# Layer 0 attention scores in 32-row tiles of TensorE, with queries and keys laid out per head through DRAM

## The reference, cut to what matters

```
xn = layernorm(x)
q = xn @ Wq.T ; k = xn @ Wk.T ; v = xn @ Wv.T        # q: 256 wide, k and v: 64 wide
qh = q.reshape(b, s, 4, 8, 8)                        # 4 queries per kv head, 8 heads, head width 8
kh = k.reshape(b, s, 8, 8)
scores = einsum('bsqhd,bthd->bqhst', qh, kh) * 8**-0.5
a_dot = einsum('bqhst,bthd->bsqhd', softmax(scores), vh)
sigma_q = elu(q) ; a_mem = sigma_q @ memory / (sigma_q @ memory_norm)
x = x + a_dot * (1 - w) + a_mem * w + ffn(xn)        # ffn: 256 -> 2048 -> 256, 4-bit weights
```

## Time and profile before

| | |
|---|---|
| median of the timed runs | 842.98 us |
| the profiled execution, its own time | 845.34 us |
| its span, first to last instruction | 843.4 us |
| PE busy | 741.0 us (88%), 5602 matmuls |
| PEld busy | 637.2 us (76%) |
| DVE busy | 632.9 us (75%) |
| ACT busy | 468.3 us (56%) |
| POOL busy | 424.2 us (50%) |
| mean granted TensorE clock | 0.953 of 2.4 GHz |

### The profile page before, as it was taken

The page is one execution under the profiler, slowest core; times in us unless marked ns, Lnnn a source line. Parts: engine busy times, 40 slices in busy tenths (PEclk is TensorE's granted clock), DMA queues, the critical chain, the costliest instruction groups (busy, mean ns, idle before and its releaser), DMA issues. The chain is left out here.

```text
span 843.4 us, 15160 instructions
## 1 busy us (share of the span) xinstructions
PE 741.0 (88%) x5602; PEld 637.2 (76%) x5602; DVE 632.9 (75%) x1099; ACT 468.3 (56%) x746; POOL 424.2 (50%) x369
## 2 busy tenths in 40 slices
PE   3368799999999999999999999999788898889773
PEld 2256678888888887888888888888666687777562
DVE  6989877787777676677768768665264898989865
ACT  4246645655655665564665565657675555565411
POOL 2344354354356566657535434436546373764821
PEclk9579999999999999999999999999979999999985
DMA  5111121111011010110100000021100000000000
GB/s 157 28 39 39 39 77 47 35 50 46 3 33 38 23 40 24 49 40 26 27 10 14 22 2 21 21 78 39 40 14 0 1 1 26 1 26 1 1 26 25
DMA packets 22108, 25.89 MB, mean 31 GB/s; under 512 B 4498, under 2 KB 17170, under 8 KB 22036
## 3 DMA queue, kind: packets, MB, share of 16 engines
q1 hardware_dynamic: 22036, 24.93, 10.4%
HBM read 14.83 MB, written 3.28 MB: 21 GB/s over the span
## 5 line engine op out<-in xcount | busy, mean ns | idle before, releaser
L652 DVE TENSOR_REDUCE neg_max<-s_pair 128x4 f32<-128x1024 f32 x127 | 154.9, 1220 | 75.5 <-PE s_pair L866 75.3
L474 ACT ACTIVATE probs<-t_pair 128x1024 f32<-128x1024 f32 x128 | 131.3, 1025 | 136.4 <-PE t_pair L891 136.2
L371 POOL TENSOR_TENSOR hid<-g,hid 128x512 f32<-128x512 f32 x64 | 82.1, 1283 | 177.8 <-DVE g L763 144.7
L365 POOL TENSOR_TENSOR hid_lo<-hid,hid_hi 128x512 fp32r<-128x512 f32 x64 | 85.5, 1336 | 82.8 <-ACT hid_hi L497 82.7
L866 PE MATMUL s_pair<-K,Q 96*128 96x256 f32 x508 | 85.0, 291 | 15.6 <-DVE neg_max L652 9.3
L866 PEld LDWEIGHTS s_pair<-K,Q 96*128 96x128 f32 x508 | 75.8, 195 | 24.2 <-issue 8.1
L891 PE MATMUL t_pair<-Q,K 104*128 104x512 f32 x256 | 86.2, 418 | 0.3 <-DMA Q<-max_parts 0.3
L933 PE MATMUL down<-hi,hid_hi 128*128 128x256 f32 x256 | 83.9, 328 | 0.8 <-POOL hid_lo L365 0.8
L906 PE MATMUL misc<-probs,V 128*32 128x256 f32 x1024 | 69.4, 389 | 3.3 <-DVE kc L608 2.6
L933 PE MATMUL down<-lo,hid_hi 128*128 128x256 f32 x256 | 71.5, 279 | 0.0
L933 PE MATMUL down<-hi,hid_lo 128*128 128x256 f32 x256 | 71.3, 278 | 0.0
(11 more groups left out here) (258 smaller groups left out, 1964.8 us busy)
## 6 DMA issues: line engine op xcount, KB each, us to landing
stage<-in_ternary SPq DMA_DIRECT2D x18, 256.0 KB, 2.8
Q<-q_hi SPq DMA_DIRECT2D x64, 64.0 KB, 2.0
stage<-in_scales SPq DMA_DIRECT2D x8, 384.0 KB, 3.4
X<-in_x SPq DMA_DIRECT2D x8, 256.0 KB, 4.2
Q<-q_lo SPq DMA_DIRECT2D x32, 64.0 KB, 2.0
Q<-max_parts SPq DMA_DIRECT2D x128, 4.0 KB
out<-X SPq DMA_DIRECT2D x8, 256.0 KB, 2.2
signs<-w_stage SPq DMA_DIRECT2D x9, 128.0 KB, 1.8
```

Source lines behind the costliest of these rows:

```text
L365: pool.tensor_tensor(hid_lo[:, m % 2, :, :].rearrange("p a n -> p (a n)"), hid[:, m % 2, :], hid_hi[:, m % 2, :, :].rearrange("p a n -> p ...
L371: pool.tensor_tensor(hid[:, m % 2, :], g[:, m % 2, :], hid[:, m % 2, :], ALU.mult).then_inc(S["hid_done"], 1)
L474: act.activation(probs[:, u % 2, th, :], t_pair[:], ACT.Exp, scale=SCALE).then_inc(S["probs_done"], 1)
L652: dve.tensor_reduce(neg_max[:, u % 2, 4 * jp:4 * jp + 4], score_banks(u, jp)[:].rearrange("p (s n) -> p s n", n=SEQ), AX_X, ALU.max, negat ...
```

## The change

Queries and keys are laid out per head. `Q[:, head, :]` and `K[:, head, :]` hold, for query r of the head, 24 rows from partition 32 r on, and two more rows for the maxima. A matmul reads only the 24 (or 26) rows of one block, a 32-row tile of the array, and `scores` and `scores_turned` issue their four matmuls so that two tiles alternate, each writing to a PSUM bank of its own. No rows of other heads take part, so the masks on POOL, `hq_mask` and `max_rows` go. `scores_turned` now covers two queries for all 256 keys with four matmuls of 256 columns, where it covered four queries for 128 keys with two of 512.

SBUF-to-SBUF copies cannot make that layout in few DMAs, so the parts of queries and keys are first stored to DRAM (`store_queries`, six DMAs, `store_keys`, one) and then loaded (`place_heads`, eight DMAs per quad, four for Q and four for K). The maxima of a unit are placed by four DMAs where there were two. The weights' columns are reordered on the host (`by_dim`).

```diff
-    for kind in ("stats", "norm", "turn", "q", "qlow", "kv", "qload0", "mask0", "qload1", "mask1"):
+    for kind in ("stats", "norm", "turn", "q", "qlow", "kv", "qstore", "kstore", "load0", "load1"):
...
-        for n, kind in (..., (4 + late, "qlow"), (4 + late, "qload0"), (4 + late, "kv"),
-                        (5, "mask0"), (5, "recip0"), (6, "recip1"), (8, "qload1"), (8, "mask1")):
+        for n, kind in (..., (4 + late, "qlow"), (4 + late, "qstore"), (4 + late, "kv"), (4 + late, "kstore"),
+                        (5 + late, "load0"), (5, "recip0"), (6, "recip1"), (8, "load1")):
...
-        Q = sb("Q", [P, 2, QPK, SEQ], F32R)
-        K = sb("K", [P, 2, QUAD, SEQ], F32R)
+        Q = sb("Q", [P, HEADS, SEQ], F32R)
+        K = sb("K", [P, HEADS, SEQ], F32R)
...
+            def store_queries(b):
+                sp.wait_ge(S["q_parts"], 3 * b + 1)
...
+                for part, x in ((0, q_hi), (2, q_hi), (1, q_lo)):
+                    if part == 1:
+                        sp.wait_ge(S["q_lo_done"], b + 1)
+                    for jj in range(2):
+                        dst = dram["q_parts"][b % 2, jj::2, DKV * part:DKV * part + DKV, :].rearrange("c e n -> e c n")
+                        sp.dma_start(dst.bitcast(F32), x[DKV * jj:DKV * jj + DKV, :, :].bitcast(F32)).then_inc(S["q_stored"], 16)
+            def store_keys(b):
+                sp.wait_ge(S["kc_lo_done"], b + 1)
...
+                sp.dma_start(dram["k_parts"][b % 2].bitcast(F32), kc[0:KROWS, :, :].bitcast(F32)).then_inc(S["k_stored"], 16)
+            def place_heads(b, quad):
                 if b > 0:
                     sp.wait_ge(S["st_done"], 2 * (HEADS * (b - 1) + QUAD * quad + QUAD))
+                heads = slice(QUAD * quad, QUAD * quad + QUAD)
+                sp.wait_ge(S["q_stored"], 96 * (b + 1))
+                for r in range(QPK):
+                    src = dram["q_parts"][b % 2, r].rearrange("(e h) n -> e h n", h=HEADS)[:, heads, :]
+                    sp.dma_start(Q[32 * r:32 * r + HROWS, heads, :].bitcast(F32), src.bitcast(F32)).then_inc(qk_placed[quad], 16)
...
+                sp.wait_ge(S["k_stored"], 16 * (b + 1))
+                for r in range(QPK):
+                    src = dram["k_parts"][b % 2].rearrange("(e h) q n -> e q h n", h=QUAD)[:, quad]
+                    sp.dma_start(K[32 * r:32 * r + HROWS, heads, :].bitcast(F32), src.bitcast(F32)).then_inc(qk_placed[quad], 16)
...
             def place_max(u):
-                if u > 0:
-                    sp.wait_ge(S["st_done"], 2 * u)
-                for part in range(2):
+                if u >= HEADS:
+                    sp.wait_ge(S["st_done"], 2 * (u - HEADS) + 2)
+                for s in range(2):
+                    for part in range(2):
...
-                elif kind in ("mask0", "mask1"):
-                    pool.tensor_tensor(K[0:KROWS, quad, :, :], src, mask, ALU.mult).then_inc(k_masked[quad], 1)
...
             def scores(u, jp):
                 if jp == 0 and hq == 0:
-                    pe.wait_ge(q_placed[quad], 96 * (b + 1))
-                    pe.wait_ge(k_masked[quad], b + 1)
+                    pe.wait_ge(qk_placed[quad], 128 * (b + 1))
...
-                for j in range(2):
-                    for s in range(2):
-                        mm = pe.matmul(score_banks(u, jp)[:, 512 * j + SEQ * s:...], Q[0:KROWS, quad, 2 * jp + j, P * s:P * s + P],
-                                       K[0:KROWS, quad, hq, :], start=True, stop=True)
+                for s in range(2):
+                    for j in range(2):
+                        rows = slice(32 * (2 * jp + j), 32 * (2 * jp + j) + HROWS)
+                        mm = pe.matmul(score_banks(u, jp)[:, 512 * j + SEQ * s:...], Q[rows, h, P * s:P * s + P], K[rows, h, :], start=True, stop=True)
...
-            def scores_turned(u, th):
-                rows = slice(0, KROWS + MROWS)
-                for jp in range(2):
-                    mm = pe.matmul(t_pair[:, 512 * jp:512 * jp + 512].rearrange("p (j n) -> p j n", j=2), K[rows, quad, hq, P * th:P * th + P],
-                                   Q[rows, quad, 2 * jp:2 * jp + 2, :], start=True, stop=True)
+            def scores_turned(u, jp):
+                for th in range(2):
+                    for j in range(2):
+                        rows = slice(32 * (2 * jp + j), 32 * (2 * jp + j) + HROWS + MROWS)
+                        mm = pe.matmul(t_pair[:, 512 * j + SEQ * th:...], K[rows, h, P * th:P * th + P], Q[rows, h, :], start=True, stop=True)
```

More of the change, by code:

```diff
@@ L60 @@
 KROWS = 3 * QUAD * DH
-MROWS = 2 * QUAD
+HROWS, MROWS = 3 * DH, 2
 CW = WORDS // 2
@@ L178, in layer0 @@
         S = {n: ctx.enter_context(nc.semaphore(f"a_{n}")) for n in names}
-        q_placed, k_masked = ([S[f"{n}{i}"] for i in range(2)] for n in ("q_placed", "k_masked"))
+        qk_placed = [S[f"qk_placed{i}"] for i in range(2)]
         stage_sem = [S[f"stage{i}"] for i in range(2)]
@@ L399, in _ @@
                 for kind, n in at.get(u, []):
-                    if kind == "mask1" and u == FIRST:
+                    step(kind, n)
+                    if kind == "qlow" and u == FIRST:
                         weights_low(0)
-                    step(kind, n)
                     if kind == "recip0" and u == -1:
@@ L429, in step @@
                     if b > 0:
-                        for quad in range(2):
-                            act.wait_ge(k_masked[quad], b)
+                        act.wait_ge(S["k_stored"], 16 * b)
                         act.wait_ge(S["v_turned"], b)
@@ L446, in query_parts @@
                 if b > 0:
-                    for quad in range(2):
-                        act.wait_ge(q_placed[quad], 96 * b)
+                    act.wait_ge(S["q_stored"], 96 * b)
                     act.wait_ge(S["sigma_done"], 2 * b)
@@ L455, in query_parts @@
                 act.activation(q_neg[:], q_neg[:], ACT.Relu, scale=-2.0).then_inc(S["q_parts"], 1)
-            def max_rows(quad):
-                rows = slice(KROWS, KROWS + MROWS)
-                own = hq_mask[rows, :].rearrange("p (h a) -> p h a", a=1).to_broadcast([MROWS, QUAD, SEQ])
-                act.activation(Q[rows, quad, :, :], own, ACT.Copy, scale=0.0).then_inc(S["rows_set"], 1)
-                act.activation(K[rows, quad, :, :], own, ACT.Copy).then_inc(S["rows_set"], 1)
             def weights_high(n):
@@ L1941, in layouts, with by_dim @@
     e = QUAD * DH
-    parts = [wq]
+    def by_dim(w, h):
+        return w.reshape(P, KC, -1, h, DH).swapaxes(3, 4).reshape(P, KC, -1)
+    parts = [by_dim(wq, HEADS)]
     for quad in range(2):
         at = slice(e * quad, e * quad + e)
-        parts += [wk[:, :, at]] * 3 + [wv[:, :, at]]
+        parts += [by_dim(wk[:, :, at], QUAD)] * 3 + [wv[:, :, at]]
     a["wqkv"] = np.concatenate(parts, axis=2)
-    a["memory"] = f["L0_attn_memory"]
-    a["memory_norm"] = f["L0_attn_memory_norm"]
+    a["memory"], a["memory_norm"] = (f["L0_attn_" + n].reshape(HEADS, DH, -1).swapaxes(0, 1).reshape(DKV, -1) for n in ("memory", "memory_norm"))
     a["memory_weight"] = f["L0_attn_memory_weight"]
-    c = np.zeros((P, P + QUAD), np.float32)
-    c[:, 0:P] = np.eye(P)
-    for row in range(KROWS):
-        c[row, P + row % e // DH] = 1.0
-    a["const"] = c
-    for hq in range(QUAD):
-        c[KROWS + 2 * hq:KROWS + 2 * hq + 2, P + hq] = 1.0
+    a["const"] = np.eye(P, dtype=np.float32)
     def by_chunk(g):
```

82 lines of the change are left out of this document (37 added, 45 removed).

## The result

| | before | after |
|---|---|---|
| median of four runs, taken in turn | 844.88 us | 862.24 us |
| ratio, 95% interval | | 1.0211 (1.0166 to 1.0257) |
| profiled execution, its span | 845.3, 843.4 us | 862.5, 860.7 us |
| mean granted TensorE clock | 0.953 | 0.940 |

The kernel is 2.1% slower (1.7 to 2.6%). The forecast was 875 us, 3.8% slower: the direction is right and the time lies in the range, but the sum is 13 us too high, and as a difference to before it is 32 us where 17.4 were measured. The terms show more than that: the largest one, +21 us for TensorE's steady part, did not come at all, and the waits for loads cost four times what I gave them.

A forecast was written before the change was run, and what follows sets the result against it. TensorE's stream bounds the kernel from about 100 to 600 us, DVE the start. 845.3 + 21 + 5 + 8.5 + 3 - 5.5 = 877.3, less 2.4 for the median: 875 us, 3.8% slower; own range 862 to 888, wider range 852 to 908.

The forecast's parts named there:

- TensorE's steady part: Units 7 to 63, from about 100 us on: mode changes outweigh side-by-side gains, 0.37 us longer per unit, +21 us in all.
- the waits for loads: Batches 2 to 7: TensorE waits 0.5 us for queries and keys before first scores, six times, +3 us (0 to 9).
- Rival A: Attention groups: row tiles do not run side by side because weight loads queue up; +82 in place of +21, 936 us; chance 0.09.
- B: Steady part: changing between full array and row tiles is cheap, under 0.18 us; at nothing, 793 us; chance 0.10.
- Rival C: Every batch: TensorE waits for loads and the clock falls behind each, +18, about 893 us, up to 905; chance 0.13.
- Rival D: Steady term's halves cancel (change costs 0.18), start and batch 1 partly hidden behind DVE's work: 843 to 850 us; chance 0.06.
- the start: First scores come 6.6 us later, behind stores and eight loads; 1.4 returns without POOL's mask: +5 us (2 to 9).
- batch 1: Its first scores wait for loads issued behind unit 7's maxima, +7.7 us, plus about 1 for the clock: +8.5 (7 to 11).
- the waits for POOL: Mem step in two batches: without masks, TensorE's 1.5 us waits for POOL's sigma and the half clock behind go, -5.5 us.
- six changes a unit, 6 x 0.24 = 1.43 us: Three attention places per unit: entering and leaving row tiles costs 0.24 us more per change, 1.43 us per unit.
- 1.07: Attention groups: gain per unit in us from tiles side by side, 0.24 + 0.24 + 0.59, with eight neighbouring matmuls in three steps.
- a period under 7.7 us: Sign in TensorE's timeline: a unit takes 7.7 us before, 8.05 by forecast; anything under 7.7 would prove the main step wrong.

## Why the prediction was right and wrong

**Right: the mechanism and its place.** Tiles run side by side (e.g. 303.50 and 303.51; 0.23 us per stretch by the kernel with both queries in one tile), the changes of mode eat that gain, and what makes the kernel slower is the longer way of the data to Q and K. Rival A (936) was refuted by the period, and so was B at its full size (793): a change is not free, it costs 0.19, just above the 0.18 at which B would begin. Rival C did not come in full (below). Rival D had two halves: the first, a cheaper change of about 0.18 and a steady part that cancels, is what came; the second, a start and a batch 1 hidden behind DVE, is not, and so its 843 to 850 did not come either.

**Right in size:** the start (+5.7 for +5), batch 1 (+8.8 for +8.5; first scores at 121.89, predicted about 122), the waits for POOL (-5.1 for -5.5). Two of these are partly luck. For batch 1 the text's own times, 115.8 and 107.84, are 8.0 apart and not 7.7. For POOL the parts named, two waits of 1.5 and a half clock of 1.7, make 4.7 with one fall of the clock and 6.4 with two; the trace before has one, since from 396 to 398, behind the second wait, the granted clock was 1.00. The POOL term also hid a condition: it assumed that nothing else would delay POOL, but the loads in SP's queue do.

**Wrong, the mis-sized step: "six changes a unit, 6 x 0.24 = 1.43 us", and against it 1.07.** Both numbers were off, in the same direction. A change costs 0.19, not 0.24: the next weight load comes 0.21 behind the last start, and I took the 0.25 of the fp32 transposes of L842. The nearest other row, the 32-column group entered at 0.21, stood there as a bound, with +14. I chose the row for its likeness in rows, and did not look whether its gap is there without a change of mode. It is. Timeline of PE before, where transposes on the full array follow the gate product:

```profile
210.26 0.40 PE L794 MATMUL gate<-xn_lo,hi 128*128 128x256 f32 x2
210.63 0.66 PE L825 MATMUL misc<-ident,xn 128*128 128x128 f32 x4
```

The last gate start is 210.38, so 0.25 again, and L848, also on the full array, has it too (184.82, behind a last start at 184.57). The 0.25 belongs to the entry into these fp32 steps, whatever makes it, and not to the tiles: rival B's "the drain may be its" was a fair doubt. And the double stretch takes two steps, not three: I counted eight matmuls in the order of the code, in pairs, and TensorE does not keep to that order between tiles. 6 x 0.05 + 0.12 = 0.42 us per unit, over 57 units 24 us; the sharing with L847, 0.35 seven times, and the 1.0 of the masks I had not seen. That is the way from +21 to -4.5, to within 2 us.

The Trainium skill, "TensorE: Matmul & The Clock Gate", section "Part 3: Packing small matmuls — row/col tiling", says that matmuls start and end in program order. Here the trace disagrees: by the code all four of L894 come before those of L871, and in the rows two of L871 start at 303.51, ahead of two of L894 at 303.72; and the kernel with tiles a, a, b, b takes the same time.

**Wrong: "a wait of 0.5, six times: +3".** The waits are 0.7 to 1.6 us, 7.4 in all, and the units lost 12.6. I set the unit's slack from one batch, 315.1 against 313.88 + 0.6. In this very unit, with the 14.64 us by which the kernel after runs late there taken off, PE comes to the wait at 313.97 and gets K at 315.56: half a microsecond is the slower stream that did not come, the other half is K, there that much later than priced.

With the wait of 1.59 at 330.20 the granted clock in the next two windows was 0.67 and 0.50, near, and this unit lost 3.48. The same happened behind the wait of 1.49 at 469.20 (0.66 from 470 to 472, 0.50 from 472 to 474; the unit lost 3.41). Behind the other four waits, of 0.7 to 1.4 us, the granted clock stayed at 1.00 and the units lost 0.1 to 0.5 us more than the wait. Rival C named the price of a fall in every batch, 18; two of six came. Of the 12.6 - 7.4 = 5.2 us beyond the waits the two falls are 3.4, each 1.7 by the windows as in the prediction; the other 1.8 I did not separate.

The two errors have opposite signs, 25.5 too much and 9.6 too little, so that the total came nearer than its parts is luck. The text had said what would show this: a period under 7.7 us disproves the main step. It was 7.65.

## What to carry to other kernels

Row tiles pay by the stretch, not by the matmul: a stretch costs two changes of mode, some 0.37 us, and a group of four 256-column matmuls in two tiles gives back 0.23. So put all work of one tiling next to each other before judging a layout; here that made 862 us into 817 together with the next point. In a queue that issues in order, look at each added DMA for what is small and urgent behind it. And when a price comes from a neighbouring row, look first whether the same gap stands also where the thing to be priced is absent.

## What the runs showed of the hardware

- A change between the full array and 32-row tiles: the next weight load 0.20 to 0.21 us behind the last start of a 256-column fp32r matmul, and 0.10 us of that load exposed; 0.19 us in all, the same in and out (0.37 per added stretch). An entry into the fp32 steps L825, L842 and L848 comes 0.25 behind the last start, on the full array too.
- Matmuls of different row tiles start out of the order of the code: eight in four tiles in 0.44 us between 303.50 and 303.94, and a, a, b, b costs what a, b, a, b costs (862.8 and 862.2 us).
- SP takes 0.38 us to issue a load of 24 partitions by four heads of Q and 0.8 for one of K; with 128 partitions one load of Q takes 0.37 and one of K 0.57, and they land after 4.8 and 5.5.
- The granted clock fell to 0.50, 1.2 GHz, behind PE waits of 1.59 and 1.49 us in the kernel after, and not behind one of 1.38 there, one of 1.49 (394.06) in the kernel before, or one of 1.70 (320.36) in the kernel with one stretch in place of two.
